# Attention values for a pair of heads in equal rounds, row sums by transposes, residual rows with four tokens a partition

## The reference

```python
q_lat = q @ q2l_w.T + q2l_b            # 8 channels a head to 32 latent ones
k_lat = k @ kv2l_w.T + kv2l_b
v_lat = v @ kv2l_w.T + kv2l_b
q_lat = q_lat * cos + _rotate_half(q_lat) * sin
k_lat = k_lat * cos + _rotate_half(k_lat) * sin
q_for_k = q_lat @ wqk_w.T + wqk_b
att = jnp.einsum('bhql,bhkl->bhqk', q_for_k, k_lat) * L ** (-0.5)
att = jnp.where(causal[None, None], att, -jnp.inf)
att = jax.nn.softmax(att, axis=-1)
y_lat = jnp.einsum('bhqk,bhkl->bhql', att, v_lat)
...
x = x + attention(xn) + ffn(xn)
```

## Time and profile before

| | us |
|---|---|
| median of 3 runs | 689.43 (689.4 to 689.87) |
| the profiled execution | 689.03 |
| its span, first to last instruction | 687.3 |
| prologue, to about | 143 |
| attention, to about | 584 |
| experts, the rest | 103 |

### The profile page before, as it was taken

The page is one execution under the profiler, slowest core; times in us unless marked ns, Lnnn a source line. Parts: engine busy times, 40 slices in busy tenths (PEclk is TensorE's granted clock), DMA queues, the critical chain, the costliest instruction groups (busy, mean ns, idle before and its releaser), DMA issues. The chain is left out here.

```text
span 687.3 us, 13300 instructions
## 1 busy us (share of the span) xinstructions
PE 613.9 (89%) x3770; PEld 416.9 (61%) x3770; DVE 488.1 (71%) x1698; ACT 374.4 (54%) x912; POOL 379.3 (55%) x476
## 2 busy tenths in 40 slices
PE   5689999279999999999999999999999997599993
PEld 4467777145565556656555655655565554499992
DVE  5468674367888878888887888887776661677772
ACT  5773342125766666667576567666666664433220
POOL 8100768554665665556666556656653221267775
PEclk9899999658999999999999999999999999699997
DMA  8515964676687686777776677866657604833333
GB/s 272 186 61 183 279 209 134 142 158 143 138 185 174 136 178 136 149 174 171 158 167 132 148 160 182 185 146 134 123 111 181 144 19 160 256 27 34 31 33 27
DMA packets 58118, 99.06 MB, mean 144 GB/s; under 512 B 7072, under 2 KB 36640, under 8 KB 57792
## 3 DMA queue, kind: packets, MB, share of 16 engines
q1 hardware_dynamic: 50384, 89.61, 55.7%
q0 software_dynamic: 7376, 7.55, 6.4%
q10 hardware_dynamic: 288, 1.05, 0.5%
HBM read 27.47 MB, written 19.87 MB: 69 GB/s over the span
## 5 line engine op out<-in xcount | busy, mean ns | idle before, releaser
L1108 ACT ACTIVATE prob<-bank 128x512 f32<-128x512 f32 (+3 forms) x512 | 210.6, 435 | 133.6 <-PE bank L1220 133.3
L1319 DVE CUSTOM_DVE_ANT_0 scratch<-bank,late 128x512 bf16<-128x512 f32 (+3 forms) x512 | 228.5, 489 | 55.0 <-PE bank L1205 48.4
L1080 POOL TENSOR_SCALAR_AFFINE_SELECT prob<-prob 128x256 f32<-128x256 f32 x256 | 104.5, 408 | 178.1 <-ACT prob L1108 176.3
L1205 PE MATMUL bank<-KQ 96*128 96x256 f32 (+2 forms) x512 | 165.4, 398 | 2.1 <-DVE mx L1319 0.9
L1205 PEld LDWEIGHTS bank<-KQ 96*128 96x128 f32 x512 | 86.3, 193 | 105.0 <-issue 61.6
L1220 PE MATMUL bank<-KQ 98*128 98x256 f32 (+2 forms) x512 | 139.0, 346 | 5.6 <-DMA KQ<-mxT 3.7
L1173 PE MATMUL bank<-prob,v_all 128*18 128x256 f32 (+3 forms) x1024 | 105.5, 439 | 0.4 <-POOL prob L1080 0.2
L1220 PEld LDWEIGHTS bank<-KQ 98*128 98x128 f32 x512 | 88.4, 191 | 24.6 <-DMA KQ<-mxT 7.7
L1412 POOL DMA_INDIRECT out<-ye,token x38 | 59.2, 1558 | 32.1 <-DVE ye L1536 26.4
L1189 PE MATMUL bank<-stk,wl 96*128 96x512 f32 x120 | 53.2, 443 | 15.0 <-PEq L271 7.5
L341 POOL DMA_INDIRECT sorted_x<-xn,pos x32 | 32.6, 1019 | 51.8 <-DVEq L796 43.0
(11 more groups left out here) (170 smaller groups left out, 986.1 us busy)
## 6 DMA issues: line engine op xcount, KB each, us to landing
KQ<-dkq SPq DMA_DIRECT2D x192, 256.0 KB, 4.2
stk<-latent SPq DMA_DIRECT2D x48, 256.0 KB, 4.4
latent<-qkH SPq DMA_DIRECT2D x8, 512.0 KB, 2.8
latent<-qkL SPq DMA_DIRECT2D x8, 512.0 KB, 4.1
x<-in_x SPq DMA_DIRECT2D x12, 256.0 KB, 4.5
sorted_x<-pad_sb POOLq DMA_DIRECT2D x10, 260.0 KB, 5.2
xs<-sorted_x SPq DMA_DIRECT2D x5, 520.0 KB, 8.8
dkq<-in_w SPq DMA_DIRECT2D x1, 2464.0 KB, 9.2
```

Of the source, the lines that this page charges most:

```text
L1080: nc.gpsimd.affine_select(out=diag, in_=diag, compare_op=ALU.is_ge, fill=0.0, base=0, pattern=[[0, 2], [1, P]], channel_multiplier=-1).the ...
L1108: nc.scalar.activation(prob[:, n % 2, cell, at:at + PW[j]], ST[i % 2][:, lo - q0:T - q0], ACT.Exp, scale=SCALE).then_inc(exp_done, 1)
L1205: nc.tensor.matmul(S[k % SBANKS][:, 0:w], KQ[0:KROWS, 1, m % SLOTS, T * b + P * q:T * b + P * (q + 1)], KQ[0:KROWS, 0, m % SLOTS, T * b:T ...
L1319: nc.vector.tensor_tensor_reduce(scratch[:, i % 2, 0:w], S[k % SBANKS][:, 0:w], mask[:, T - w:T], 1.0, MASKED, ALU.add, ALU.max, mx[:, m % ...
```

## The change

1. **Values.** `v_all` holds 18 blocks of 9 columns for each tile of tokens (values and a one for each head, then the router's logits), no zeros between. GpSimd sets only the ones, in one memset instead of two.
2. **Rounds.** The value products of steps n-2 and n-1 are issued together in steps n (even) and n+1: a round is one key tile with two batches and two heads, so four products with the same number of columns, each with 9 columns of weights and with a row group of `Y` for itself. Key tile 2 comes in slot 1 and 3 in slot 3 of the even step, 1 in slot 0 and 0 in slot 2 of the odd one. `prob` has four buffers instead of two.
3. **Row sums.** Nothing needs adding any more, so the four products with `sumsel` become four transposes of `ysb`. They are issued in slot 1 of odd steps (before: slot 2), two steps later than before; DVE reads them at place 5 (before: 7).
4. **The end of 16 heads** comes two steps later (`turn_part`), `out_part` moves on TensorE from slot 1 to slot 3 and on DVE from place 3 to place 7. SP's store moves from n mod 16 = 6 to 8, its load from 7 to 9. LAST is two steps later.
5. **Residual rows.** A partition of `xres` holds four tokens in a row (2 KB in `out`) instead of four tokens 128 apart; `yT` is read with a step of four.

```diff
-                nc.gpsimd.memset(v_all[:], 0.0).then_inc(v_clear, 1)
-                pool.wait_ge(v_clear, 1)
-                v_pairs = v_all[:].rearrange("p t c w -> p (t c) w")
-                nc.gpsimd.memset(v_pairs[:, :, HD:VP:2 * VW], 1.0).then_inc(v_clear, 1)
+                nc.gpsimd.memset(v_all[:, :, :, HD], 1.0).then_inc(v_clear, 1)
...
-    prob = sb("prob", [P, 2, QT, PCOLS], F32)
+    prob = sb("prob", [P, 4, QT, PCOLS], F32)
...
     def turn_part(n):
-        pair, part = (n - 18) // H, (n - 18) % H
+        pair, part = (n - 20) // H, (n - 20) % H
...
     def row_sums(n):
-        return (n - 3) // 2 if n % 2 == 1 and 3 <= n <= STEPS + 1 else None
+        pair = (n - 5) // 2
+        return pair if n % 2 == 1 and 0 <= pair < STEPS // 2 else None
+
+    def values_of(n):
+        pair = n // 2 - 1
+        return pair if 0 <= pair < STEPS // 2 else None
...
-                if n % H == 6 and 0 <= n - H < STEPS:
+                if n % H == 8 and 0 <= n - H < STEPS:
...
-                if n % H == 7 and 0 <= n < STEPS:
+                if n % H == 9 and 0 <= n < STEPS:
...
-                        if i == 0 and n >= 2:
-                            act.wait_ge(pv_done, n - 1)
+                        if i == 0 and n >= 4:
+                            act.wait_ge(pv_done, n // 2 - 1)
...
-            def pv(m, tiles, first, final):
...
-                pe.wait_ge(cut_done, 4 * m + 4)
-                for j in tiles:
-                    for b in range(2):
-                        q = 2 * b + (j in (1, 2))
...
+            def value_round(pair, j, first, final):
+
+                batches, head = 2 * pair // H, 2 * pair % H
+                if first:
+                    if pair:
+                        pe.wait_ge(y_copied, pair)
+                    else:
+                        pe.wait_ge(y_clear, 1)
+                    pe.wait_ge(cut_done, 8 * pair + 8)
+                c0 = T - PW[j]
+                for b in range(2):
+                    cell, at = prob_at(b, j)
+                    for hp in range(2):
+                        q = 2 * b + hp
+                        last = nc.tensor.matmul(Y[L * q:L * q + VW, c0:T],
+                                                v_all[:, 2 * QT * batches + QT * b + j, head + hp, :],
+                                                prob[:, (2 * pair + hp) % 4, cell, at:at + PW[j]],
+                                                start=first, stop=final, skip_group_check=True)
...
-                    if slot == 2 and pair is not None:
+                    if slot == 1 and pair is not None:
                         pe.wait_ge(y_copied, pair + 1)
                         m_free()
-                        Z = M[:, 0:2 * YW * QT].rearrange("p (b q c) -> p q b c", b=2, q=QT)
+                        Z = M[:].rearrange("p (b q c) -> p q b c", b=2, q=QT)
                         for q in range(QT):
-                            last = nc.tensor.matmul(Z[:, q], ysb[:, P * q:P * (q + 1)],
-                                                    sumsel.rearrange("p (b c) -> p b c", b=2), start=True, stop=True,
-                                                    skip_group_check=True)
+                            last = nc.tensor.transpose(Z[:, q], ysb[:, P * q:P * (q + 1)], ident)
...
-                    if slot == 0 and 0 <= n - 1 < STEPS:
-                        pv(n - 1, (2, 3), True, False)
-                    if slot == 3 and 0 <= n - 1 < STEPS:
-                        pv(n - 1, (0, 1), False, True)
+                    pair = values_of(n)
+                    if (n % 2, slot) == (0, 1) and pair is not None:
+                        value_round(pair, 2, True, False)
+                    if (n % 2, slot) == (0, 3) and pair is not None:
+                        value_round(pair, 3, False, False)
+                    if (n % 2, slot) == (1, 0) and pair is not None:
+                        value_round(pair, 1, False, False)
+                    if (n % 2, slot) == (1, 2) and pair is not None:
+                        value_round(pair, 0, False, True)
...
-                    if i == 3 and pair is not None:
+                    if i == 7 and pair is not None:
...
-                    if i == 7 and pair is not None:
-                        Z = M[:, 0:2 * YW * QT].rearrange("p (t h c) -> p t h c", t=2 * QT, h=2)
+                    if i == 5 and pair is not None:
+                        Z = M[:].rearrange("p (t h c) -> p t h c", t=2 * QT, h=2)
```

More of the change, by code:

```diff
@@ L37 @@
 VW = HD + 1
-YW = 2 * VW
-VP = 3 * VW
-VC = 9
+VB = H + 2
 PW = [T - P * j for j in range(QT)]
@@ L1018, in _ @@
                         sp.wait_ge(mixed_out, 16 * pair)
-                    sp.dma_start(xres[:], out[PT * pair:PT * (pair + 1), :].rearrange("(t p) c -> p t c", p=P)
+                    sp.dma_start(xres[:].rearrange("p (f t) c -> p f (t c)", f=2), out[PT * pair:PT * (pair + 1), :].rearrange("(f p t) c -> p f (t c)", f=2, t=QT)
                                  ).then_inc(xres_in, 16)
@@ L1115, in _ @@
                         nc.scalar.copy(mxT[:, m % 2, 0, :], MXT).then_inc(mxT_high, 1)
-                    pair = row_sums(n + 1)
-                    if i == 7 and pair is not None:
-                        act.wait_ge(pv_done, n)
+                    pair = values_of(n)
+                    if i == 7 and n % 2 == 1 and pair is not None:
+                        act.wait_ge(pv_done, pair + 1)
                         if pair:
@@ L1238, in _ @@
                         issued["yt"] += 1
-                    pair, f = out_part(n)
-                    if slot == 1 and pair is not None:
-                        m_free()
-                        for t in range(QT):
-                            last = nc.tensor.matmul(M[:, C * t:C * (t + 1)], yT[:, P * t:P * (t + 1)], wout[:],
-                                                    start=True, stop=True, skip_group_check=True)
-                        last.then_inc(out_ready, 1)
-                        issued["o"] += 1
                     wG, wf = latent_product(n)
```

69 lines of the change are left out of this document (29 added, 40 removed).

## The result

The change makes the kernel slower. In the runs on one chip the kernel before took 689.41 us (median; 687.7 to 689.87) and the changed one 711.42 us (705.95 to 716.38): a ratio of 1.031, with a 95% interval of 1.027 to 1.036. The forecast was 687.8 and its range ended at 693.

What follows compares the result with a forecast made beforehand. TensorE, busy 89%, was taken to be held by waits for VectorE's buffers and, every fourth step, by the maxima's landing. From 689.0 us the terms -2.0 - 3.2 - 1.8 + 4.2 + 1.6 = -1.2 gave 687.8; range 680 to 693.

Steps and rivals of the forecast that it cites:

- The load of `xres`: SP's queue: the load, now ahead of already late maxima, costs 1.4 us in each of three batch pairs: +4.2 us.
- rival C: Slower: the `xres` load costs 2.4 us and also pushes the next step's fill: 691 us; chance 0.10.
- rival E: TensorE, with less to do, falls to 1.2 GHz in the last six pairs: +38 us, 726; chance 0.03.
- The ring: Slot 1's second score waits for the buffer that slot 0's 512 maxima on VectorE free: new 0.9 us a pair.
- Rival B: Slower: the wait for VectorE's buffer is 1.2 us instead of 0.9, in 19 pairs: 693.5 us; chance 0.13.
- rival A: The 0.9 us wait for VectorE's buffer isn't there, because VectorE catches up: 671 us; chance 0.12.
- ACT behind L1251: In even steps ACT's two copies, 0.69 us each, delay the last 512 exponential: 0.3 us a pair on average.
- Pairs without a landing: Thirteen pairs of steps before step 52 take 12.7 us, 0.15 less than before: -2.0 us.
- Pairs with a landing: Thirteen pairs of steps whose length the maxima's transfer sets gain 0.25 us each: -3.2 us.
- Late pairs: The six following pairs, without projections, gain 0.3 us each: -1.8 us.
- `yT` with a step of four: Output products read `yT` with a step of four: 32 products, costed at nothing.
- The end: Behind the last exponential, rounds of 2.61 us and a row sum of 0.45 replace 1.27 of value products: +1.6 us.

Runs made afterwards that it cites:

- experiment 2: Kernel before with the load of `xres` at n mod 16 = 9, behind the latents, instead of 7: 719.66 us, ratio 1.029.
- experiment 3: Kernel before with the load at 9 and four unread products where TensorE stands still in steps 11, 27 and 43: 709.08 us, ratio 1.014.
- experiment 10: Changed kernel with latents loaded in three parts and row sums by two-pass products with the identity instead of transposes: 703.89 us, ratio 1.006.
- experiment 6: Latents loaded in three parts over three steps, `xres` load at 12 in the changed kernel (691.23 us, 0.988), at 8 in the kernel before (695.68 us, 0.995).
- experiment 8: Changed kernel with the load at 11 and ACT's copy ordering `yT` so weights are read without a step: 695.64 us, ratio 0.993.
- experiment 11: Changed kernel with the load at 11, ACT's ordered copy of `yT`, latents unsplit, and maxima issued ahead of the fill: 714.04 us, ratio 1.022.
- experiment 4: Changed kernel with half of the `xres` load (256 KB) at n mod 16 = 9 and half at 11: 713.36 us, ratio 1.020.
- experiment 1: Changed kernel with the load of `xres` at n mod 16 = 11 instead of 9: 701.72 us, ratio 1.0046.
- experiment 9: Changed kernel with latents loaded in three parts and the division behind slot 3's maxima on VectorE (place 7 instead of 5): 708.06 us, ratio 1.013.
- experiment 7: Changed kernel with latents loaded in three parts and ACT's copy ordering `yT` so weights are read without a step: 686.92 us, ratio 0.983.

## Why the prediction was wrong

**The load of `xres` is the step that failed.** It was a term of its own, +4.2 us, with the right place and the right steps (11, 27, 43), and rival C named its price of up to 2.4 us each. In the changed kernel the three places cost 14.8 us, and the same move alone costs the kernel before 21. Two things were missing.

- The size of the delay. 512 KB at 355 GB/s were to take 1.4 us. The way from the latents' issue to the landing of the maxima took 10.3, 9.9 and 9.7 us before at steps 11, 27 and 43, and 11.6, 14.5 and 11.8 after: 1.3, 4.6 and 2.1 us more, and 3.9, 2.2 and 3.3 more in experiment 2. The 355 GB/s came from a stretch of 1 us in which small pieces ran; at the 222 GB/s of the crowded stretch the upper bound was 2.4, and three of the six passed that too. In all of them SyncE issued the next fill (339.33 above) before the maxima had landed, but so it did in the kernel before, too (at step 31: 359.89 against 362.06). What differs is the spread: the 16 pieces of 512 bytes of step 27's maxima began between 341.5 and 345.1 (the last landed at 346.3), those of step 31 in the kernel before within 0.6 us (359.8 to 360.4). Why they were pulled apart, and what part of the extra the next fill has, stays open.
- The clock. I had put rival E on transposes and work that thins out, with 0.03. It fell, but for another reason: a stop for a transfer, with nothing for TensorE to do. In the changed kernel stops of 3.1, 6.0 and 3.2 us are followed by stretches at 1.2 GHz, and the steps behind them took 7.4, 8.6 and 7.5 us where 5.9 to 6.0 is usual: 5.7 us together. The Trainium skill, TensorE: Matmul & The Clock Gate, section "HAM oscillation — how this bites in real kernels", describes just this chain, a wait for a transfer, a lower clock and a cold next piece of work; experiments 2 and 3 agree with it (10.2 us against 6.4 for the step behind the stop). That page was open to me, and I weighed only its part on transposes. With four transposes in every pair the changed kernel's granted clock stays at 1.00 up to the last transposition of the maxima where nothing stops TensorE, so by that part nothing happened there; and experiment 10, with products in place of the transposes, had two short falls of its own (below).

The stop was dangerous only because the landing already made TensorE wait, in eight of thirteen such steps. The prediction says that faster products don't shorten it; it didn't say that they lengthen the idle time ahead of it. Before, TensorE waited 0.5 us there and its clock held; with the load added it waited for 2 to 6.

**Point by point.**

- Rounds and row sums: right. 0.97, 0.76, 0.55 and 0.33 us were forecast, 0.98, 0.76, 0.55 and 0.34 measured; the row sums 0.45 and 0.36.
- The ring: right in place, 0.6 us instead of 0.9. Rival B (1.2) and rival A (none) are both out.
- ACT behind L1251: right. The second of slot 0's two transposed score products (256 columns) stands 0.49 us behind the first (386.99 to 387.48) where 0.23 is usual in the kernel before.
- Pairs without a landing: 12.46 us instead of 12.7 (before 12.94 there, 12.70 to 12.33 early on), so 0.4 to 0.5 less, not 0.15. The ring's wait was 0.3 shorter than forecast, and I had kept another 0.1 in reserve. Experiment 10 shows the path that sets them.
- Pairs with a landing: from 31 to 33 it was 13.59 and is 13.15, so 0.44 less instead of 0.25. But only eight of the thirteen that I had counted have a landing that makes TensorE wait (experiment 6).
- Late pairs: 11.77 before and 10.80 after (two steps from transposition 60 to 62), so 1.0 less, not 0.3.
- `yT` with a step of four, costed at nothing as "32 products": wrong by 5.1 us in attention, and the step from the last division to the last addition of `xres` at the end took 5.7 us instead of 3.8. Counting instructions was right, but each one's weight load grew from 192 to 329 ns. This is the second term that failed.
- The end: +1.6 us forecast from the last exponential to the last copy of `Y`; 2.5 became 4.3, so 1.9. (The terms of the prediction give 2.61 + 0.45 - 1.27 = 1.8, not 1.6.) The last exponential itself stands 1.6 us farther behind the last transposition of the maxima, 11.2 us instead of 9.6, which I hadn't seen. The granted clock is at 1.2 GHz from 581.8 to 588.6 there, where the kernel before has it full until 585.3, behind its attention's last products. In three variants of the changed kernel whose clock held there (experiments 8, 10 and 11) the same way took 9.2 us, so it is the clock and not the order. The experts' part took 2.3 us less (100.7 against 103.0) though nothing in it was changed; over all 14 traces it lies between 100.7 and 103.3, so I take this for the spread of single executions.
- The memset: nothing, as forecast. The first transposition is 0.5 us later.
- A stop at step 3, forecast nowhere: in the changed kernel it lasted 3.5 us, with a lower clock behind it, 4.1 us in all. The maxima landed at 178.5, 1.6 us later than before, and TensorE was 1.3 us earlier. Experiments 4, 8 and 11 had it at step 3 (3.9, 2.5 and 2.4 us), 1, 6 and 9 at step 2 instead (1.7, 2.4 and 1.7), all with the same fall behind it; 7 and 10, the kernel before and its variants had none over 1.1 us and no fall. It is the same kind of stop, but why most variants of the changed kernel have it wasn't tried.

Put together: the forecast's gains came, and more (10.3 us against 7.0), and 27.2 us of losses stood against them (24.1 in attention's stages, 2.6 behind them, 0.5 ahead) where 5.8 were forecast. The order of the products is sound. The load's place and the strided weights undo it.

## What to carry to other kernels

When a stage waits for a landing, cost what is put ahead of that landing by the idle time that it leaves on TensorE and not by the bytes alone: once TensorE stood still for over 2 us, the step behind the stop ran at 1.2 GHz, and that was 5.7 of 14.8 us in the changed kernel and 11 of 21 in experiment 2. Look at the queue's order before the engines' order; moving one load by two steps was worth 2.7%, and splitting a burst over three steps another 1.6%. And a view with a step in it was free here for ACT's copy and dear for a weight load: ask which operand it is, and put the step where it costs nothing. Last, a saving on TensorE counts only where it stands on the path of the pair: the row sums' did, the rounds' was lost in the wait for VectorE.

## What the runs showed of the hardware

- A weight load of 128 columns of float32 with a step of four elements (16 bytes) took 329 ns against 192 in a row; a product with it 397 against 275. ACT's copy from the bank `M` with the same step took 585 ns, as without it.
- Behind all stops of TensorE of 2.1 to 6.0 us for a landing the rows show 1.2 GHz for 3 to 10 us. Shorter stops went both ways: behind one of 1.1 us (experiment 1, step 11) the clock stayed at 2.4 GHz, behind one of 1.2 us (experiment 8, step 27) it fell. Between 170 us and the last transposition of the maxima the clock of the kernel before and its variants fell only with the load at 9. The changed kernel and its variants each fell at least once, and two of them without a stop of 1 us ahead of the fall: experiment 10 at 309 and 326 us, with no wait over 0.63 us in the 8 us before, and experiment 9 at 434 and 543 us (0.76 and 0.99). The two steps at those falls in experiment 10 took about 1.5 us more than in experiment 6 (8.47 and 8.01 against 6.94 and 6.64). Behind the last transposition both kinds fell. So rival E holds a grain of truth for the thinner kernel, by a few us and not by its 38; what sets off these falls stays open.
- Products that nobody reads kept the clock up: 3.6 us of them in each of three stops made the kernel 1.5% faster.
- The changed kernel's runs spread over 1.5% (705.95 to 716.38), those of the kernel before over 0.3% in the same set. In the four executions of the changed kernel the mean granted clock lay between 0.918 and 0.940. On one of the other chips the kernel before spread over 1.4% (694.43 to 703.84), so part of that may be the chip's.
